# Near one-hot rows of a graph network layer: relu(1 - |node - destination|) on ScalarE in two steps in place of one comparison on VectorE

## What is computed

```
h = relu(layernorm(x))
e = concat(h[src], h[dst])                      # per edge, 128 features
g1 = lrelu(e @ gate_w1.T)   for 4 heads of 64
m1 = lrelu(e @ msg_w1.T)    for 4 heads of 128
a = pos[dst] * exp(lrelu(g1 @ gate_w2.T))
beta = lrelu(m1 @ msg_w2.T)
x = x + mean over heads of segment_sum(a / segment_sum(a)[src] * beta, src)
```

## Time and profile before

| | value |
|---|---|
| median of three runs | 6369.76 us |
| profiled execution, its own time | 6382.29 us |
| its span, first to last instruction | 6380.7 us |
| busy share: TensorE, VectorE, ScalarE, GpSimd | 70%, 73%, 41%, 56% |
| mean granted TensorE clock | 0.785 of full speed |

### The profile page before, as it was taken

The page is one execution under the profiler, slowest core; times in us unless marked ns, Lnnn a source line. Parts: engine busy times, 40 slices in busy tenths (PEclk is TensorE's granted clock), DMA queues, the critical chain, the costliest instruction groups (busy, mean ns, idle before and its releaser), DMA issues.

```text
span 6380.7 us, 112465 instructions
## 1 busy us (share of the span) xinstructions
PE 4448.9 (70%) x25026; PEld 2772.9 (43%) x25026; DVE 4638.8 (73%) x10169; ACT 2628.9 (41%) x6414; POOL 3558.8 (56%) x3640
## 2 busy tenths in 40 slices
PE   5799999999999999999999723333344443344443
PEld 4455555555555555555555323333333333333333
DVE  3488888888888888888888766666666666666664
ACT  3666667666666666666666510000000000000000
POOL 0255555555555555555555355656656556666664
PEclk8999999999999999999999855555555555555555
DMA  7533333333333333333333322222222222222222
GB/s 195 184 75 74 75 76 74 75 75 75 74 75 73 77 73 74 75 75 75 75 75 75 87 81 42 44 43 44 44 42 43 43 43 43 47 44 43 44 44 39
DMA packets 484894, 436.01 MB, mean 68 GB/s; under 512 B 294336, under 2 KB 366240, under 8 KB 483744
## 3 DMA queue, kind: packets, MB, share of 16 engines
q0 software_dynamic: 122512, 173.81, 15.7%
q1 hardware_dynamic: 334416, 247.54, 14.7%
q10 hardware_dynamic: 27840, 13.23, 1.1%
HBM read 363.28 MB, written 70.96 MB: 68 GB/s over the span
## 4 chain that ended last, share of the span: by engine, by line
PE 39%; issue 25%; DVE 10%; POOL 6%; SPq 6%; DMA 5%; ACT 4%; another core or an unknown queue 4%; DVEq 1%; ACTq 0%; POOLq 0%
PE ps_beta L1922 12%; PE ps_hidden L1870 8%; PE ps_hidden L1871 7%; POOL work L827 4%; DVE work L1358 3%; PE ps_sum L1941 3%; POOL ends L827 3%; PE ps_beta L1930 3%; PE ps_alpha L1904 1%; DMA attn_quads<-in_edge_weight 1%; SPq L592 1%; DMA ends<-src_table,src_quads 1%; PE ps_alpha L1913 1%; ACT beta_scaled L969 1%
## 5 line engine op out<-in xcount | busy, mean ns | idle before, releaser
L774 POOL DMA_INDIRECT ends<-split_table,src_pairs x1612 | 1578.0, 979 | 1615.7 <-issue 1459.6
L827 POOL DMA_INDIRECT work<-src_table,src_quads x808 | 806.8, 998 | 856.4 <-DMA attn_quads<-in_edge_weight 361.8
L1870 PE MATMUL ps_hidden<-ends_parts,w_high 128*128 128x512 f32 x2418 | 1097.4, 454 | 159.2 <-ACT ends_hot L964 60.0
L1358 DVE TENSOR_TENSOR work<-work,ps_hidden 128x512 f32<-128x512 f32 x1612 | 1101.0, 683 | 54.7 <-ACT work L911 43.5
L2107 PE MATMUL ps_beta<-work,equal 128*128 128x128 f32 x1616 | 411.4, 435 | 904.8 <-DVE work L1785 540.2
L911 ACT ACTIVATE work<-ps_hidden 128x512 f32<-128x512 f32 x1612 | 947.2, 600 | 219.3 <-PE ps_hidden L1871 179.6
L1871 PE MATMUL ps_hidden<-ends_hot,window 128*128 128x512 f32 x2418 | 954.5, 395 | 4.1 <-issue 3.8
L827 POOL DMA_INDIRECT ends<-src_table,src_quads x804 | 802.7, 998 | 257.9 <-issue 244.1
L1363 DVE TENSOR_TENSOR beta<-beta_scaled,ps_beta 128x512 f32<-128x512 f32 x806 | 551.4, 684 | 418.1 <-ACT beta_scaled L969 346.5
L1132 ACT ACTIVATE ps_alpha<-dots 128x8 f32<-128x8 f32 x403 | 72.4, 180 | 1876.9 <-DVE dots L1746 1336.8
L2107 PE MATMUL ps_beta<-work,dst_rows_sb 128*128 128x128 f32 x1608 | 411.4, 437 | 609.6 <-DVE work L1785 430.1
(11 more groups left out here) (202 smaller groups left out, 6703.2 us busy)
## 6 DMA issues: line engine op xcount, KB each, us to landing
window<-window_table SPq DMA_DIRECT2D x403, 192.5 KB
parts<-in_edge_attr SPq DMA_DIRECT2D x101, 512.0 KB
dst_rows_sb<-in_dst_rows SPq DMA_DIRECT2D x403, 128.0 KB
ends<-split_table,src_pairs POOLq DMA_INDIRECT x1612
window_table<-parts SPq DMA_DIRECT2D x49, 386.0 KB
sums<-key_rows POOLq DMA_DIRECT2D x403, 32.6 KB
work<-src_table,src_quads POOLq DMA_INDIRECT x808
ends<-src_table,src_quads POOLq DMA_INDIRECT x804
```

What stands on the lines that cost most here:

```text
L774: pool.indirect_dma_start(out=ends[m][:, t, :], out_offset=None, in_=split_table, in_offset=bass.IndirectOffsetOnAxis(ap=src_pairs[m // 2] ...
L827: pool.indirect_dma_start(out=ends1_windows[m][:, t, :], out_offset=None, in_=src_table, in_offset=bass.IndirectOffsetOnAxis(ap=src_quads[ ...
L1358: nc.vector.tensor_tensor(hidden[k][:, :], scaled[k % NL][:, :], ps_hidden[k % NL][:, :], ALU.max).then_inc(hidden_ready, 1)
L1870: nc.tensor.matmul(o, w1_high[:, k * P:(k + 1) * P], ends_parts[j][:, :], start=True, stop=False)
```

## The change

The match moves from VectorE's program to ScalarE's and becomes two instructions. `step_near` computes |node - destination| (function Abs, scale -1, the node as a bias read per partition) into a spare buffer `near_steps`, and `match_near` computes relu(1 - that) with a bias of 1 read per partition, which for whole numbers is 1 where they are equal and else 0. In ScalarE's block `step_near(b+1)` stands between chunks 2 and 3 and `match_near(b+1)` between chunks 3 and 4, ahead of `copy_ends(b+1)`. A semaphore `near_stepped` orders the two. For the bias the tile `ones` grows from one row to 128. For block 0 both stand ahead of the first `copy_ends`.

```diff
-        ones = sb("ones", [1, P])
+        ones = sb("ones", [P, P])
+        near_steps = key_rows[1][D:P, :, :].rearrange("p t e -> p (t e)").bitcast(F32)
+        near_stepped = sem("near_stepped")
+            def step_near(b, half, j):
+                act.wait_ge(window_in[j], 32 * (half + 1))
+                nc.scalar.activation(near_steps, dst_rows_sb[j][D:P, :, :].rearrange("p t e -> p (t e)"), ACT.Abs,
+                                     bias=window[j][D:P, HID:HID + 1].bitcast(F32), scale=-1.0).then_inc(near_stepped, 1)
+            def match_near(b, j):
+                act.wait_ge(near_stepped, b + 1)
+                wait(act, hidden_done, NK * (b - 1))
+                nc.scalar.activation(ends_hot[j][D:P, :], near_steps, ACT.Relu, bias=ones[D:P, 0:1],
+                                     scale=-1.0).then_inc(hot_T_ready, 1)
                 scale_chunk(b, 2)
+                if not is_final(b):
+                    step_near(b + 1, half + j, 1 - j)
                 scale_chunk(b, 3)
+                if not is_final(b):
+                    match_near(b + 1, 1 - j)
                 scale_chunk(b, 4)
+            act.wait_ge(fits_step, 1)
+            step_near(0, 0, 0)
+            match_near(0, 0)
             copy_ends(0, 0)
-            def match_near(b, half, j):
-                dve.wait_ge(window_in[j], 32 * (half + 1))
-                wait(dve, hidden_done, NK * (b - 1))
-                nc.vector.tensor_scalar(ends_hot[j][D:P, :], dst_rows_sb[j][D:P, :, :].rearrange("p t e -> p (t e)"),
-                                        window[j][D:P, HID:HID + 1].bitcast(F32), None,
-                                        ALU.is_equal).then_inc(hot_T_ready, 1)
                 rectify_chunk_windows(b, 2)
-                if not is_final(b):
-                    match_near(b + 1, half + j, 1 - j)
                 rectify_chunk_windows(b, 3)
-            match_near(0, 0, 0)
```

More of the change, by code:

```diff
@@ L995, in edges0_windows @@
             def edges0_windows(b, quad, m):
-                j = m % 2
+                half, j = 2 * quad + m // 2, m % 2
                 if not (isinstance(b, int) and b == 0):
@@ L1393, in edges0_windows @@
             def edges0_windows(b, quad, m):
-                half, j = 2 * quad + m // 2, m % 2
                 begun = not (isinstance(b, int) and b == 0)
@@ L2029, in _ @@
             pe.wait_ge(firsts_ready, 2)
-            nc.tensor.matmul(ps_sum[:, 0:NB], ones[:, :], first_dst[:, :], start=True,
+            nc.tensor.matmul(ps_sum[:, 0:NB], ones[0:1, :], first_dst[:, :], start=True,
                              stop=True).then_inc(firsts_spread, 1)
-            nc.tensor.matmul(ps_hidden[2][:, 0:NB], ones[:, :], near_dst[:, :], start=True,
+            nc.tensor.matmul(ps_hidden[2][:, 0:NB], ones[0:1, :], near_dst[:, :], start=True,
                              stop=True).then_inc(firsts_spread, 1)
```

## The result

The changed kernel takes 6905.06 us (median of four runs, 6884.6 to 6925.02), the kernel before 6369.69. The ratio is 1.0827 (95% interval 1.0798 to 1.0856), 535 us more where 287 were forecast. The profiled execution of the changed kernel took 6925.02 us, 542.7 more than that of before. The forecast had the right sign and the right place, about half the size, and the time lies outside the stated range.

A forecast was written before the change was run, and what follows sets the result against it. A ring through TensorE's pair product, ScalarE's queue and `ends_hot` was taken to bound the kernel. Terms of 2.85 us in four blocks, times 100.75 quads, gave 287 us more: 6657 us, range 6470 to 6830.

The forecast's parts named there:

- a ring with 0.1 to 0.6 us to spare: Block loop: pair product, ScalarE's queue, `ends_hot`, products 0 and 1, pair product; slack 0.61 (m = 3) to 0.09 us (m = 1).
- VectorE's relief worth nothing: Removing VectorE's 0.49 us comparison per block was to save no time, even in m = 1, where `ends_hot` becomes late instead.
- Durations of the new instructions: Each of the two added ScalarE instructions of 64 x 512 elements was to last 0.70 us.
- Their distances: Start-to-start cost of the two new ScalarE instructions, neighbours overlapping: 0.60 us each, 1.20 a block.
- upper end of 1.40 us a block: High case for the two ScalarE instructions: 0.70 us each, no overlap.
- the sum: Added ScalarE time less idle time and TensorE slack: m = 3 0.30, m = 0 0.84, m = 1 1.11, m = 2 0.60 us.
- the DMA wait: In m = 0, `step_near` on ScalarE waits for the destinations' load: 0.77 less 0.30, so 0.47 us.
- m = 2, where a gap in ScalarE was to take in `step_near`: ScalarE's 1.60 us idle between chunks 2 and 3 absorbs `step_near`; only `match_near`'s 0.60 us is added.
- the term for m = 1: Block m = 1, ScalarE back to back after `sum_quad`: 1.20 us added less 0.09 slack, 1.11 us.
- table load: Rival: Abs or Relu outside Exp's set forces two loads a block, up to 1034 us more, about 7690; chance 0.03.
- The clock: Rival: TensorE's granted clock falls in the first layer, up to 3000 us more, even a tenth being 300; chance 0.03.
- a sign of being wrong: Signs named: waits at `ends_hot` that don't grow, new table loads, or granted clock under 1.00 between 250 and 3500 us.

## Why the prediction was right or wrong

*The bound, a ring with 0.1 to 0.6 us to spare:* right. In the ring one instruction costs 4%, in the idle time outside it nothing.

*VectorE's relief worth nothing:* right for this kernel, with dead work beside the comparison the time is the same (1.0831 against 1.0827). TensorE's waits for chunk 3 did go, 47.3 to 2.3 us, and came back as waits for the copy.

*Durations of the new instructions:* 0.70 forecast, 0.72 measured.

*Their distances:* this is the term that failed. The step was "neighbours overlap", taken from copies and from instructions that all start at partition 0, and its upper end of 1.40 us a block assumed no overlap behind the new instructions alone. It is 1.89: the overlap is lost ahead of each new one, behind each, and at Exp. That adds 0.69 in each of four blocks, 2.76 a quad, 278 us, and the sum with it and without the DMA wait would be 2.85 + 2.76 - 0.47 = 5.14 us in four blocks, 518 us, against the 525 measured in the loop.

That closeness is partly luck. TensorE's waits for the copy and for VectorE's chunk grew from 102.0 us in 357 blocks to 428.3 in 308, that is 1.10 us a block or 445 us in all, less than the 518. The rest is TensorE's own busy time, which grew from 8.04 us a block (2869.21 in 357) to 8.2 (2540.74 in some 309), 75 to 85 us:

```profile
500.00:3500.00 3000.00, 2869.21 (x17828) 1567.57 (x17825) 2545.47 (x4993) 2065.04 (x4728) 1725.77 (x1785) 1.00 0.35 75
...
500.00:3500.00 3000.00, 2540.74 (x15419) 1378.91 (x15416) 2100.01 (x4010) 2292.47 (x4705) 1495.18 (x1544) 0.98 0.30 65
```

(the kernel before, then the changed one). The falls of the clock, which the sum doesn't hold, can account for most of it: 40 x 1.69 = 68 us. Over all 128 partitions the distances are those of the forecast and the time is close to it, 273 us more than before against 287. There too only about 190 us stand in these waits (249.1 us in 331 blocks), so the sum's terms for single blocks weren't all right.

*The DMA wait:* 0.47 us forecast in m = 0. In the changed kernel there is none to speak of (L971 idles 7.9 us in 309), probably because the longer ring gives the load more time. Over 128 partitions it shows, 42 waits, 23.8 us:

```profile
ACT key_rows L973 <- DMA dst_rows_sb<-in_dst_rows: 23.8, 42, 0.9
```

*m = 2, where a gap in ScalarE was to take in `step_near`:* wrong. TensorE's wait there grew from 0.80 to 2.31 us, the most of all (m = 1 1.21, m = 3 1.20, m = 0 0.98). The gap still exists once in four blocks, but now ahead of `scale_pair(b-1, 1)`, and nothing is absorbed:

```profile
2010.93 0.19 ACT L1001 ACTIVATE alpha_scaled<-ps_alpha 128x16 f32<-128x16 f32 x1
2012.47 0.60 ACT L984 ACTIVATE beta_scaled<-ps_beta 128x512 f32<-128x512 f32 x1 [1.35 <-remote]
```

In both kernels this wait ends long after the matmul that it is for: the last of the pair's ended at 2010.78, 1.69 us before the copy here, and before the change product 3 ended at 2042.93, 1.78 us before chunk 3 started at 2044.71. The cause of that delay wasn't found; no run tried it. With the distances put right the sum has 1.29 us more in m = 2, where the wait grew by 1.51, and 1.80 more in m = 1, where it grew by 0.86 (from 0.35): the term for m = 1 was too large, and its error covers that of m = 2.

*The rivals:* no table load (the trace after has the same single one for Exp's line), as the Trainium skill's page ScalarE: Activation LUTs, Table sets: the hidden batching unit, says. The clock was given 0.03 and, even at a tenth, 300 us; it did come under 1.00, which the prediction had named as a sign of being wrong, but small: filling the waits gave back 31 us.

The Trainium skill describes the lost overlap on another engine's page: VectorE: DVE Perf Modes, Two Vector instructions with no wait between them, says that an instruction whose operand starts in another quadrant of 32 partitions than the last operand in the same memory did waits until all earlier ones have finished. That rule is given for Vector instructions; the distances here on ScalarE agree with it at the only two starts that were tried, 0 and 64, with 0.12 to 0.15 us lost each time.

## What to carry to other kernels

A low busy share says little about where an engine has room: find the ring that bounds the loop and the one place where the engine waits in it. Price an inserted instruction by the distance from the one before to the one after, not by its duration, and take that distance from rows with the same start partition; if half the partitions are needed, starting at partition 0 and computing all of them can be the cheaper form. The most that this bought here was half the loss: no form of the change beat the kernel before.

## What the runs showed of the hardware that was not expected

On ScalarE, copies of 512 elements that start at partition 0 follow each other in 0.48 to 0.50 us though each lasts 0.60. One that starts at partition 64 between them is 0.60 to 0.62 behind the one before, and the next comes 0.65 to 0.66 (plain copy) or 0.74 to 0.75 (bias per partition) later, against 0.61 for the latter when it starts at 0. An instruction reading SBUF at partition 0 after one that read it at 64 is delayed as well, even with copies from PSUM between them: Exp 0.62 to 0.65 instead of 0.47 to 0.50. Falls of the granted clock from 1.00 to 0.50, some 3 us long, appeared with TensorE's waits of 1 to 2.3 us a block (40 in 403 blocks) and went, all but one, when 0.7 us of each wait was filled with dead matmuls.
